# First attention of a four-layer network: value products ahead of the products for the maxima

## The chip, the cores and the metric

The kernel runs on one core of a Trainium2 chip. The metric is the device time of one execution in microseconds. A core has five engines with a program each: TensorE (PE, its weight loads are listed apart as PEld), VectorE (DVE), ScalarE (ACT), GpSimd (POOL) and SyncE (SP), which here only issues DMAs. The engines meet at semaphores alone, and each works through its program in the order in which it is written. TensorE writes to PSUM, which has eight banks of 128 x 512 float32.

## The reference, cut to what matters

Four layers, each `x = x + s * silu(f)` with an attention or a recurrence for `s` and a mixture of experts or a table of weights for `f`, both from the layer norm of `x`. The change lies in the attention of the first layer (2 batches of 1024 tokens, 16 heads, 8 numbers in a query or key, 64 in a value):

```python
cp = leaky_relu(einsum('btd,cd->btc', xn, Wc) + bc)
q, k, v = ...
scores = einsum('bqhd,bkhd->bhqk', q, k) / SCALE
attn = softmax(scores, axis=-1)
out = einsum('bhqk,bkhd->bqhd', attn, v).reshape(B, T, V_DIM)
proj = leaky_relu(einsum('btv,dv->btd', out, Wo) + bo)
s = xn + proj
```

## The kernel before, in words

The first attention is a loop of 256 iterations (`SCHED`, line 53; TensorE's part in lines 835 to 867). An iteration takes one group of four heads, one pair of heads in it, 512 queries and one tile of 128 keys. Eight iterations (the eight key tiles) make a **unit**: one pair of heads and 512 queries, 32 units in all. In iteration `i` TensorE issues, in this order:

- the **scores** of iteration `i`, four bf16 matmuls of 64 x 64 x 512 into a pair of PSUM banks, lines 846 to 852. ScalarE turns the pair into exponentials in SBUF (line 1916), which empties it;
- the products for the **maxima**: the softmax subtracts a row maximum, and these are found eight iterations and more ahead, by the same scores computed a second time with the queries on the partitions. `max_pair` (743 to 760) issues four bf16 matmuls of the same shape into another pair of banks, and VectorE reduces that pair to its maxima (1260), which empties it. `searched` (663 to 668) deals out 240 such pairs: one in each iteration up to 231, a second one in eight of the first 14 iterations (`EARLY`), none after 231;
- the **values** of iteration `i - 2` (`LAG`, line 44; `pv`, 783 to 800): four float32 matmuls of 64 x 64 x 512, exponentials times values, added up over the eight iterations of a unit in banks 6 and 7. `pv` waits for the exponentials of `i - 2`, and in the first iteration of a unit's sums also for banks 6 and 7 to be emptied, by ScalarE and by VectorE;
- `tails(i)` (802 to 833): in the second iteration of a unit the row sums of the unit before (16 float32 matmuls) and mostly the projection of the unit three back (8 float32 matmuls);
- what is left of `searched(i)`, and once in two units two small transposes for the maxima (`max_rows`, 762 to 774), in the fifth iteration of odd units.

The scores and the maxima take their banks from one ring of three pairs (0, 2, 4) in the order in which they are issued: `take` (379 to 382) hands out the next pair, and `vacant` (384) waits until what filled it last has been emptied. So the scores of `i` as a rule stand in the pair that the maxima of `i - 2` had, and wait for VectorE; the maxima of `i` stand in the pair that the scores of `i - 1` had, and wait for ScalarE. The tails and the transposes take a pair of the ring too.

VectorE's loop (1331 to 1346) reduces the pair of the iteration first; then come, once in a unit, additions of the low and high half of the values (`osb`, 1290) and of the projection (`acc_sb`, 1318) in the second iteration, the scaling of a finished unit by its reciprocal sums (`on_sb`, 1305) in the third, and a small sum with a reciprocal (1296 to 1298) in the sixth. GpSimd adds up exponentials for the row sums. Beside the loop all engines have parts of the layer's experts and of the next layer's routing, dealt out by iteration in `SIDE_B` (115 to 147); on VectorE these are for instance eight additions of an expert's rows to `gT`.

Of the kernel before, what the change touches and what calls it, by code (L numbers as in the profile page):

```python
# [43 lines left out]
LAG = 2  # L44
# [297 lines left out]
class Marks:  # L342
# [19 lines left out]
    def up(self, *keys, by=1):  # L362
        name = keys[0][0]
        self.n[name] = self.n.get(name, 0) + by
        self.named(name, self.n[name], [k for k in keys if len(k) > 1])
        return self.sem(name), by
# [4 lines left out]
    def at(self, *key):  # L371
        assert key in self.place or not self.known, key
        name, n = self.place.get(key, ("none", 0))
        return self.sem(name), n
# [4 lines left out]
    def take(self, ring):  # L379
        i = self.turn.get(ring, 0)  # L380
        self.turn[ring] = i + 1
        return ring[i % len(ring)]

    def vacant(self, b):
        return self.sem(f"bank{b}_empty"), self.n.get(f"bank{b}_full", 0)

    def filled(self, b, *keys):
        name = f"bank{b}_full"
        self.n[name] = self.n.get(name, 0) + 1
        self.named(name, self.n[name], keys)  # L390
        for k in keys:
            self.bank[k] = b
        return self.sem(name), 1
# [55 lines left out]
def _program(nc, A, out, ctx):  # L449
# [213 lines left out]
    def searched(i):  # L663


        done = min(i + sum(j < i for j in EARLY), 16 * (NBL - 1))
        to = min(i + 1 + sum(j <= i for j in EARLY), 16 * (NBL - 1))
        return [(1 + t // 16, t % 16) for t in range(done, to)]

    def rows_of(i, step):  # L670

        return i // 16 + 1 if i % 16 == MS[i >= 16] + step and i // 16 + 1 < NBL else None
# [16 lines left out]
    def tensor_program(pe):  # L689
# [53 lines left out]
        def max_pair(B, m, banks):  # L743

            g, pr = B // 2, B % 2
            s, qt, hk = g % 3, m // 2, m % 2
            for b in banks if len(banks) > 1 else (banks[0], banks[0] + 1):
                pe.wait_ge(*vacant(b))
            pe.wait_ge(*at(f"stack{s}_in", g))
            for a in range(2):  # L750
                r = slice(64 * a, 64 * a + 64)
                b = banks[a] if len(banks) > 1 else banks[0] + a
                for n in range(2):
                    ins = pe.mm(ps[64 * n:64 * n + 64, b, :],
                                Qs[r, s, 2 * pr + a, 128 * qt + 64 * n:128 * qt + 64 * n + 64],
                                Ks[r, s, pr, 512 * hk:512 * hk + 512])
                if len(banks) > 1:
                    ins.then_inc(*filled(b, ("mx", B, m, a)))
            if len(banks) == 1:
                ins.then_inc(*filled(banks[0], ("mx", B, m)))  # L760

        def max_rows(B, b):
            k = B % 2
            pb = ps[:, b, :].bitcast(BF16)
            pe.wait_ge(*vacant(b))
            pe.wait_ge(*at("rows_split", B))
            if B == 0:
                pe.tr(pb[0:48, 0:128], nsp[:, 0:48], identb).then_inc(*filled(b, ("rowsT", B)))
                return
            pe.wait_ge(*vacant(b + 1))  # L770
            for n in range(2):
                r = slice(64 * n, 64 * n + 64)
                ins = pe.tr(ps[:, b + n, :].bitcast(BF16)[0:48, 0:64], nsp[r, 48 * k:48 * k + 48], identb[r, r])
            ins.then_inc(*filled(b, ("rowsT", B)))
# [8 lines left out]
        def pv(i):  # L783
            g, pr, hf, kt = SCHED[i]
            tile = 8 * (g // 4) + kt
            if kt == 0:
                pe.wait_ge(*vacant(6))
                pe.wait_ge(*vacant(7))
            pe.wait_ge(*at("exp", i))
            for n in range(2):  # L790
                r = slice(64 * n, 64 * n + 64)
                for a in range(2):
                    h = 4 * (g % 4) + 2 * pr + a
                    ins = pe.mm(ps[64 * a:64 * a + 64, 6 + n, :],
                                V0[r, 1024 * tile + 64 * h:1024 * tile + 64 * h + 64],
                                Ps[r, i % NP, 512 * a:512 * a + 512], start=kt == 0, stop=kt == 7)
                if kt == 7:
                    ins.then_inc(*filled(6 + n, ("pvd" if n else "pvd_low", i)))
            if kt < 7:
                ins.then_inc(*up(("pvd", i)))  # L800
# [29 lines left out]
        def tails(x):  # L830
            unit_tail(x // 8 - 3, x % 8 + 16)
            unit_tail(x // 8 - 1, x % 8)
            unit_tail(x // 8 - 2, x % 8 + 8)

        def attention():
            ring[0] = (0, 2, 4)
            for b in range(8):
                pe.wait_ge(*vacant(b))
            pe.wait_ge(*at("v", 0, 1))
            for i, (g, pr, hf, kt) in enumerate(SCHED):  # L840
                s, b0 = g % 3, take(ring[0])
                pe.wait_ge(*vacant(b0))
                pe.wait_ge(*vacant(b0 + 1))
                pe.wait_ge(*at("rows0_in", 2 * g + pr))
                pe.wait_ge(*at("rows1_in", 2 * g + pr))
                for a in range(2):
                    r = slice(64 * a, 64 * a + 64)
                    for n in range(2):
                        ins = pe.mm(ps[64 * n:64 * n + 64, b0 + a, :],
                                    Ks[r, s, pr, 128 * kt + 64 * n:128 * kt + 64 * n + 64],  # L850
                                    Qs[r, s, 2 * pr + a, 512 * hf:512 * hf + 512])
                ins.then_inc(*filled(b0, ("st", i)))
                pairs = searched(i)
                for p in pairs[:1]:
                    max_pair(*p, (take(ring[0]),))
                if i >= LAG:
                    pv(i - LAG)
                tails(i)
                for p in pairs[1:]:
                    max_pair(*p, (take(ring[0]),))  # L860
                if rows_of(i, AFTER[i >= 16]):
                    max_rows(rows_of(i, AFTER[i >= 16]), take(ring[0]))
                yield
            pv(254)
            pv(255)
            for x in range(256, 260):
                tails(x)
# [274 lines left out]
        def down_ffn(q):  # L1142
            layer = GROUPS[q][0]
            wide, chunks = HIDDEN[layer], HIDDEN[layer] // 128
            for J in range(FIRST[q], FIRST[q + 1]):
# [6 lines left out]
                for k in range(halves(J)):  # L1152
# [9 lines left out]
                  "ffn2": ffn2, "tile": tile, "att3": att3, "state3": state3, "end3": end3, "route": route}  # L1162
        follow(ORDER_A["tensor"], stages)
        beside(attention(), SIDE_B["tensor"], stages)
        ring[0] = (4, 6, 7)
        follow(ORDER_C["tensor"], stages)
# [1550 lines left out]
```

## Time and profile before

| what | us |
|---|---|
| median of 3 runs (lowest, highest) | 989.15 (988.64, 989.76) |
| the profiled execution, its own time | 985.0 |
| its span, from first to last instruction | 983.2 |
| first and last exponential of the loop start | 152.4 and 607.1 |
| busy in the span: PE, DVE, POOL, ACT | 894.0, 766.7, 599.2, 537.4 |

The profile shows one execution, 4.15 us below the median of the runs; 1.8 us of its time lie outside its span. Busy time of PE counts a matmul from its start to a modelled end, and matmuls overlap, so a busy PE need not be at its limit. "Idle before" is the time that an engine, or TensorE's weight loading, did nothing before an instruction, with the work whose end released it.

### The profile page before, as it was taken

What the parts mean: (1) busy time and instruction counts of PE and PEld (TensorE: products, weight loads), DVE (VectorE), ACT (ScalarE), POOL (GpSimd) and SP (SyncE); (2) the same over time, 40 slices, a digit from 0 to 9 for tenths busy, and PEclk for the clock granted to TensorE, in tenths of its full rate; (3) what the DMA queues carried; (4) which work ended last, traced back from release to release, by engine and by line L of the source; (5) the groups of instructions that cost most, each with busy time, mean ns of one, the idle gap of its engine ahead of it and who ended that gap; (6) DMA issues with size and microseconds to landing.
All of it is one profiled execution on the core that took longest, in us unless ns stands there. A gap on an engine that the chain in (4) does not pass through costs nothing. (4 is left out here: it accounts for less than half of the span.)

```text
span 983.2 us, 20738 instructions
## 1 busy us (share of the span) xinstructions
PE 894.0 (91%) x7627; PEld 471.3 (48%) x7627; DVE 766.7 (78%) x1324; ACT 537.4 (55%) x903; POOL 599.2 (61%) x533
## 2 busy tenths in 40 slices
PE   4899997999999999899998999789999778799996
PEld 2356562233333333233332233679887444478695
DVE  6997789888888888998888852894589999983413
ACT  2154455666766676566666676454365334375463
POOL 3670327668887776878698876106527787572323
PEclk9899998999999999999999999999999999999999
DMA  9362364011111201102111113548761001253562
GB/s 314 117 208 86 105 195 145 16 41 47 32 57 29 65 25 31 49 22 74 40 40 38 40 35 110 169 140 262 217 188 62 23 24 52 68 164 106 161 180 83
DMA packets 90339, 94.86 MB, mean 96 GB/s; under 512 B 23136, under 2 KB 67296, under 8 KB 89984
## 3 DMA queue, kind: packets, MB, share of 16 engines
q1 hardware_dynamic: 85120, 83.04, 27.5%
q0 software_dynamic: 5120, 10.50, 3.7%
q8 instruction: 62, 1.02, 0.4%
q14 instruction: 37, 0.30, 0.1%
HBM read 68.79 MB, written 24.25 MB: 95 GB/s over the span
## 5 line engine op out<-in xcount | busy, mean ns | idle before, releaser
L254 PE MATMUL ps<-ar 64*64 64x512 f32 (+3 forms) x5244 | 518.7, 446 | 28.1 <-DVE small L276 8.9
L254 PEld LDWEIGHTS ps<-ar 64*64 64x64 f32 (+2 forms) x5244 | 254.3, 135 | 275.7 <-ACT ar L300 84.1
L300 ACT ACTIVATE ar<-ps 128x1024 f32<-128x1024 f32 (+1 forms) x302 | 284.0, 944 | 117.5 <-PE ps L254 111.3
L276 DVE TENSOR_REDUCE small<-ps 128x2 f32<-128x1024 f32 (+2 forms) x276 | 306.6, 1139 | 46.6 <-PE ps L254 44.7
L263 POOL TENSOR_TENSOR psum_sb<-psum_sb,ar 128x1024 f32<-128x1024 f32 x91 | 214.8, 2360 | 53.1 <-DVE on_sb L263 41.9
L263 POOL TENSOR_TENSOR ar<-ar 128x512 f32<-128x512 f32 (+1 forms) x80 | 80.0, 1004 | 45.4 <-DVE ar L276 22.3
L322 POOL DMA_INDIRECT gT<-ysort,rt x48 | 48.0, 999 | 92.8 <-issue 91.5
L263 DVE TENSOR_TENSOR ar<-ps,ar 128x256 f32<-128x256 f32 (+4 forms) x48 | 50.5, 1059 | 55.2 <-PE ps L254 51.4
L263 POOL TENSOR_TENSOR psum_sb<-ar 128x1024 f32<-128x1024 f32 x32 | 75.8, 2370 | 23.8 <-ACT ar L300 16.6
L297 ACT COPY ar<-ps 128x256 f32<-128x256 f32 (+2 forms) x84 | 30.8, 378 | 72.7 <-PE ps L254 33.3
L254 PE MATMUL ps<-wA,xnT 128*128 128x512 f32 (+3 forms) x208 | 60.8, 419 | 4.0 <-DVE rt L268 1.8
L254 PE MATMUL ps<-ar,onesf 128*32 128x512 f32 x384 | 61.0, 593 | 1.4 <-DVE psum_sb L263 1.3
L254 PEld LDWEIGHTS ps<-ar,psum_sb 128*128 128x128 f32 x428 | 52.1, 192 | 7.8 <-issue 7.5
L254 PE MATMUL ps<-ar,psum_sb 128*128 x428 | 55.3, 276 | 0.2 <-DVE psum_sb L263 0.2
L297 ACT COPY lrow<-ps 128x512 f32<-128x512 f32 x32 | 18.8, 586 | 66.8 <-PE ps L254 66.8
L317 POOL DMA_INDIRECT xsort<-ar,rt x32 | 35.7, 1115 | 30.4 <-DVE rt L279 22.3
L276 DVE TENSOR_REDUCE ar<-ar 128x16 f32<-128x256 f32 (+1 forms) x48 | 49.6, 1037 | 0.7
L317 POOL DMA_INDIRECT xsort<-acc_sb,rt x32 | 35.4, 1105 | 20.3 <-DVE rt L279 10.8
L254 PE MATMUL ps<-ar,ps_sb 128*128 x92 | 46.5, 604 | 0.0
L260 PE MATMUL ps<-cf,ar 128*128 128x128 f32 x256 | 33.1, 287 | 9.3 <-DVE acc_sb L271 5.0
L254 PEld LDWEIGHTS ps<-wA,xnT 128*128 128x128 f32 x208 | 30.8, 196 | 22.1 <-issue 9.7
L260 PEld LDWEIGHTS ps<-cf,ar 128*128 128x128 f32 x256 | 30.8, 149 | 14.5 <-DVE acc_sb L271 5.6
(160 smaller groups left out, 1077.2 us busy)
## 6 DMA issues: line engine op xcount, KB each, us to landing
ar<-in_L_up SPq DMA_DIRECT2D x46, 384.0 KB, 4.0
ar<-in_L_b SPq DMA_DIRECT2D x30, 322.0 KB, 3.6
rec_sb<-lscr SPq DMA_DIRECT2D x64, 128.0 KB, 2.9
scr<-ar SPq DMA_DIRECT2D x48, 128.0 KB, 2.6
ar<-xsort SPq DMA_DIRECT2D x36, 128.0 KB, 3.9
ysort<-ar SPq DMA_DIRECT2D x36, 128.0 KB, 1.9
ar<-scr SPq DMA_DIRECT2D x32, 112.0 KB
ar<-scr SPq DMA_DIRECT2D x32, 96.0 KB
```

Of the source, the lines that this page charges most:

```text
L254: return self.e.matmul(o, l, r, start=start, stop=stop) if self.e else Nothing()
L260: return self.e.matmul(o, i, idn, start=start, stop=stop, is_transpose=True) if self.e else Nothing()
L263: return self.e.tensor_tensor(o, a, b, op) if self.e else Nothing()
L276: return self.e.tensor_reduce(o, a, AX.X, op, negate=True) if negate else self.e.tensor_reduce(o, a, AX.X, op)
L297: return self.e.copy(o, a) if self.e else Nothing()
L300: return self.e.activation(o, a, fn, **kw) if self.e else Nothing()
L317: return self.e.indirect_dma_start(rows, bass.IndirectOffsetOnAxis(ap=index, axis=0), i, None)
L322: return self.e.indirect_dma_start(o, None, rows, bass.IndirectOffsetOnAxis(ap=index, axis=0))
```

## The change

In TensorE's program the call of `pv` moves ahead of the first pair of the iteration's maxima. Which work is done, in which banks and with which semaphores stays the same (the values take no pair of the ring), and no other engine's program changes.

```diff
                 ins.then_inc(*filled(b0, ("st", i)))
                 pairs = searched(i)
+                if i >= LAG:
+                    pv(i - LAG)
                 for p in pairs[:1]:
                     max_pair(*p, (take(ring[0]),))
-                if i >= LAG:
-                    pv(i - LAG)
                 tails(i)
                 for p in pairs[1:]:
                     max_pair(*p, (take(ring[0]),))
```

## Rows read from the trace of the kernel before

**Rows 1.** Page, busy time: us (share of the span) xinstructions.
```profile
PE 894.0 (91%) x7627; PEld 471.3 (48%) x7627; DVE 766.7 (78%) x1324; ACT 537.4 (55%) x903; POOL 599.2 (61%) x533
```

**Rows 2.** Busy time by stretch: PE, PEld, DVE, ACT, POOL, clock, DMA.
```profile
198.00:560.00 362.00, 350.07 (x3884) 111.03 (x3876) 314.80 (x394) 241.12 (x281) 285.36 (x216) 1.00 0.15 42
```

**Rows 3.** ScalarE in order of time, 295 to 310 us: one unit.
```profile
295.64 1.03 ACT L300 ACTIVATE ar<-ps 128x1024 f32<-128x1024 f32 x1 [0.30 <-PE ps L254]
...
301.25 2.16 ACT L300 ACTIVATE ar<-ps 128x1024 f32<-128x1024 f32 x2
303.87 1.03 ACT L300 ACTIVATE ar<-ps 128x1024 f32<-128x1024 f32 x1 [0.46 <-PE ps L254]
305.16 1.02 ACT L300 ACTIVATE ar<-ps 128x1024 f32<-128x1024 f32 x1 [0.26 <-PE ps L254]
306.48 1.03 ACT L300 ACTIVATE ar<-ps 128x1024 f32<-128x1024 f32 x1 [0.30 <-PE ps L254]
...
309.10 1.03 ACT L300 ACTIVATE ar<-ps 128x1024 f32<-128x1024 f32 x1 [0.30 <-PE ps L254]
```

**Rows 4.** ScalarE in the last iterations of the loop, without maxima.
```profile
606.05 1.03 ACT L300 ACTIVATE ar<-ps 128x1024 f32<-128x1024 f32 x1
...
607.12 1.02 ACT L300 ACTIVATE ar<-ps 128x1024 f32<-128x1024 f32 x1
```

**Rows 5.** TensorE's weight loads in order of time, from 300 us.
```profile
300.63 0.60 PEld L254 LDWEIGHTS ps<-ar 64*64 64x64 bf16 x16 [0.84 <-issue]
...
302.33 0.39 PEld L254 LDWEIGHTS ps<-ar 64*64 64x64 bf16 x12 [0.70 <-ACT ar L300]
...
304.94 0.39 PEld L254 LDWEIGHTS ps<-ar 64*64 64x64 bf16 x12 [0.51 <-ACT ar L300]
```

**Rows 6.** VectorE in order of time, 301 to 309 us, the same unit.
```profile
301.31 1.23 DVE L276 TENSOR_REDUCE small<-ps 128x2 f32<-128x1024 f32 x1 [1.38 <-PE ps L254]
302.45 0.68 DVE L263 TENSOR_TENSOR on_sb<-osb,rec_sb 128x512 f32<-128x512 f32 x1
303.05 1.22 DVE L276 TENSOR_REDUCE small<-ps 128x2 f32<-128x1024 f32 x1
304.18 1.22 DVE L276 TENSOR_REDUCE small<-ps 128x2 f32<-128x1024 f32 x1
...
306.55 0.16 DVE L276 TENSOR_REDUCE small<-lcol 128x8 f32<-128x16 f32 x1
...
306.87 2.38 DVE L276 TENSOR_REDUCE small<-ps 128x2 f32<-128x1024 f32 x2
```

**Rows 7.** All engines, 334 to 337 us, where VectorE is late.
```profile
334.29 1.36 DVE L271 SCALAR_TENSOR_TENSOR gT<-acc_sb,rt,gT 128x128 f32<-128x128 f32 x1
...
335.57 1.21 DVE L276 TENSOR_REDUCE small<-ps 128x2 f32<-128x1024 f32 x1
...
336.83 0.60 PEld L254 LDWEIGHTS ps<-ar 64*64 64x64 bf16 x16 [1.47 <-DVE small L276]
```

**Rows 8.** VectorE by groups, 198 to 572 us: busy us, mean ns, idle before.
```profile
L276 DVE TENSOR_REDUCE small<-ps 128x2 f32<-128x1024 f32 x208 | 248.1, 1215 | 37.8 <-PE ps L254 36.2
L263 DVE TENSOR_TENSOR on_sb<-osb,rec_sb 128x512 f32<-128x512 f32 x26 | 23.9, 919 | 0.0
...
L271 DVE SCALAR_TENSOR_TENSOR gT<-acc_sb,rt,gT 128x128 f32<-128x128 f32 x8 | 6.5, 807 | 0.0
```

**Rows 9.** TensorE's weight loads behind the transposes of an odd unit.
```profile
318.40 0.11 PEld L254 LDWEIGHTS ps<-ar 64*64 64x64 bf16 x4 [0.52 <-ACT ar L300]
318.91 0.39 PEld L254 LDWEIGHTS ps<-ar 64*64 64x64 bf16 x12 [0.40 <-DVE small L276]
```

**Rows 10.** GpSimd in order of time, behind the loop.
```profile
661.87 1.09 POOL L317 DMA_INDIRECT xsort<-ar,rt  x1 [21.66 <-DVE rt L279]
```

**Rows 11.** Busy time by stretch, in the columns of rows 2.
```profile
156.00:158.00 2.00, 1.80 (x16) 0.67 (x20) 2.00 (x3) 0.74 (x1) 1.98 (x2) 0.50 0.50 159
...
402.00:404.00 2.00, 0.05 (x4) 0.05 (x8) 1.97 (x4) 0.00 (x0) 1.37 (x2) 1.00 0.00 0
```

## The prediction

> **What bounds the kernel now.** The page comes first: TensorE is busy for 91% of the span, VectorE for 78% [rows 1]. That is an average over four layers, so the second view is the busy time by stretch. In the steady part of the first attention TensorE is busy for 350 of 362 us, VectorE for 315, ScalarE for only 241 [rows 2]. Third, the iterations one by one. From the start of one exponential to the next it is 1.29 or 1.32 us where nothing else is in the way [rows 3]. In the last iterations, which have no maxima, it is 1.07 [rows 4]. So the four bf16 matmuls of the maxima take 0.22. The scores are four matmuls of the same form, 0.22 as well, and 0.86 is left for the values. These three add up to 1.29 with nothing over: in a plain iteration TensorE's issue is the limit. Fourth, what TensorE waits for. The maxima of an iteration mostly come just behind the end of an exponential: their weights are loaded 0.51 us after the load before, released by ScalarE, and 0.70 in the iteration in which ScalarE also copies the row sums [rows 5]. The excess of 0.2 there, and the 0.03 in every second plain iteration, are what the old order loses to ScalarE. VectorE is no limit yet, but it is near: a unit of 13.46 us (from 295.64 to 309.10) [rows 3] holds eight reductions, each of which keeps it for 1.13 (303.05 to 304.18) [rows 6].
>
> **What is removed and what is added.** No instruction is. The four matmuls of the values with their eight weight loads, and the signals that they give, come 0.22 earlier in an iteration; the four matmuls of the maxima come 0.86 later. No DMA is issued in either, and no queue is passed.
>
> What is gained: the maxima no longer stand behind an exponential that has only just ended. Per unit that returns the 0.2 and about three times 0.03, together 0.29. In odd units there is one more: behind the transposes the maxima wait for VectorE; their weights come 0.51 behind the ones of the scores (318.40 to 318.91) [rows 9] where 0.22 is the issue, so 0.29 more is returned, as the values are now issued during that wait.
>
> What is lost: the maxima's pair of banks goes to the scores two iterations later. In the old order TensorE issues maxima, values, scores, maxima and values between the two: 0.22 + 0.86 + 0.22 + 0.22 + 0.86 = 2.38. In the new order it is maxima, scores, values and maxima: 0.22 + 0.22 + 0.86 + 0.22 = 1.52. In that time the pair has to be filled, reduced and given back. From the start of the maxima to the start of an idle VectorE's reduction it is 0.44: scores start at 300.63, the maxima 0.24 behind them (0.22, and some 0.02 because the weights are not loaded ahead after a pause; compare 1.32 with 1.29 [rows 3]), the reduction at 301.31 [rows 5, 6]. The reduction lasts 1.22 [rows 8]. From its end to the weights of the scores it is 0.05 (335.57 + 1.21 = 336.78, then 336.83) [rows 7]. Together 1.71. **The old order has 0.67 to spare; the new one is 0.2 short**, and whatever else VectorE does in a unit comes on top, since nothing is left to absorb it. That such a wait is real is seen in the old kernel where an addition to gT of 1.36 makes VectorE late: the scores stand until the reduction ends [rows 7].
>
> **The walk through one unit**, from the scores of its third iteration (time 0), where VectorE has been idle behind the tails [rows 6]; an iteration without a wait is 1.29, the maxima start 1.07 behind the scores, and a wait costs 0.02 more for the weights, as above.
> - Third: maxima 1.07, reduction 1.51 to 2.73. Behind it VectorE does the scaling, 0.92 on average [rows 8], and starts the next reduction 0.08 before its end.
> - Fourth: scores 1.29, maxima 2.36; their reduction starts only at 2.73 + 0.92 - 2 x 0.08 = 3.49 and ends at 4.71.
> - Fifth: the scores would start at 2.58 but need the first reduction, 2.73 + 0.05 = 2.78: wait 0.20. Maxima 3.88, reduction 4.62 to 5.84.
> - Sixth: would start at 4.10, needs 4.76: wait 0.66. Maxima 5.86, reduction 6.30 to 7.52; the small sum and the reciprocal put 0.32 (306.55 to 306.87) [rows 6] behind it.
> - Seventh: 6.08, needs 5.89, no wait. Maxima 7.15, reduction 7.76 to 8.98.
> - Eighth: 7.37, needs 7.57: wait 0.20. Maxima 8.67, reduction 9.11 to 10.33.
> - First of the next unit: 8.89, needs 9.03: wait 0.14. Second: 10.35, needs 10.38: wait 0.03. Then the projection, whose pair is that of the maxima just before: 0.05.
>
> Waits 1.28, four times 0.02 for weights, 1.36 in all. Against the 0.29 returned this is **+1.07 for an even unit**. In an odd unit the transposes take one of the waits and the other 0.29 is returned: **+0.78**. The tails of about 2.8 us that follow let VectorE catch up, so nothing is carried over. Maxima run in units 0 to 28. Units 0 and 1, with the second pairs, are bound by VectorE already; I take nothing for them (bounds -2 and +3). For 14 even and 13 odd units it is 14 x 1.07 + 13 x 0.78 = 25.1. Units in which side work stands on TensorE may lose less, the eight additions to gT [rows 8] will cost more than now; I let the two cancel.
>
> The other waits of the values: in a unit's third iteration they also need banks 6 and 7, emptied by VectorE's addition of osb, and the maxima are now queued behind that wait. It ends about 2.3 us after the maxima before it (0.44, one reduction, the addition), and the tails put some 3.1 us between, so I take nothing; without that cover it would be up to 0.7 per unit. The values need the exponentials of two iterations back, long done. After the loop the next layer's tokens are sorted only when VectorE has finished with the attention's output: GpSimd idles for 21.66 us before it [rows 10]. So what the loop loses, the end loses.
>
> The sum goes against the profiled execution, 985.0 (span 983.2 and 1.8 around it): 1010.1. The median of the runs is 4.15 above it, so I forecast 989.15 + 25 = **1014 us**.
>
> Bounds. Low: only the three bare shortages of 0.2 per unit, less 0.29, for 27 units: 0.3 x 27 = +8, 997. High: all VectorE's extra work in the chain paid on top of 0.2 for every two iterations (0.7 + 0.84 + 0.32, less 0.29, is 1.57 per unit, 42 in all): 1031.
>
> **TensorE's clock** is where a rule speaks for another size. The rows: the granted clock is 1.00, the higher level of 2.4 GHz, over the whole steady stretch [rows 2], also in a stretch of 2 us with TensorE busy for 0.05 [rows 11]; at the loop's start, after a pause, it was 0.50, the 1.2 GHz level [rows 11]. The Trainium skill (TensorE: Matmul & The Clock Gate, A second HAM failure mode: psum-queue depth-cycling) says that TensorE cycling through PSUM banks with small idle times between groups can make its clock swing between the levels, which would be the third rival below instead of no cost. By rows 11 the trace speaks against it here.
>
> **Rivals.**
> 1. Faster: the pair comes back in time after all, because the reduction waits less for TensorE than the 0.44 that I read; it decides at 0.44 - 0.2 = 0.24 us. Then only what is returned counts: 14 x 0.29 + 13 x 0.58 = 11.6, 978 us. For it: ScalarE's release is what ends most of the maxima's waits now [rows 5]. Against it: 0.44 was read with VectorE idle. 4%.
> 2. A wash: the returned waits and the shortage cancel within 2 us, 989. It needs VectorE's scaling and small sums to find room in the tails, while rows 6 show them in the middle of the unit. 5%.
> 3. The clock falls for a tenth of the loop, 36 us at half speed, so 36 more: 1050. 2%.
> 4. More is lost: side work on VectorE and longer scalings fall into the chain in full, the high bound, 1031. For it: gT's 1.36 in rows 7. 12%.
>
> **How the numbers follow.** The forecast has 77%. Slower is the forecast with rivals 3 and 4, 91%; the same is rival 2, 5%; faster is rival 1, 4%. A difference under 0.2%, about 2 us, can't be told from none. The range takes in the forecast's bounds, from 997 to 1029, and leaves rivals 1, 2 and 3 and half of 4 outside.
>
> **What would show it.** Right: idle time of weight loads that reductions (DVE small) end grows by some 25 us or more in the loop while that ended by ScalarE shrinks; the start of the maxima is no longer late; units of about 14.5 us where 13.46 stood, with one iteration of about 1.9; VectorE idle behind TensorE between reductions. Wrong: units of 13.2, or waits at the values; a granted clock under 1.00 in the loop; a loop that got longer while the end did not move.

## The result, and the profile after

The changed kernel takes 1009.58 us (median of 4 runs, 1007.91 to 1011.51), the kernel before beside it 989.0: a ratio of 1.0206, with a 95% interval from 1.0183 to 1.023. It is slower by 20.6 us; 25 were forecast. The profiled execution took 1007.91, the fastest of the four, with a span of 1006.1. All times of "after" below are of that execution.

The page and the busy time by stretch come first, as [rows 1, 2] did. The columns of the stretch are those of rows 2.

```profile
PE 909.5 (90%) x7627; PEld 477.5 (47%) x7627; DVE 764.6 (76%) x1324; ACT 534.6 (53%) x903; POOL 595.9 (59%) x533
```

```profile
198.00:576.00 378.00, 358.85 (x3888) 111.85 (x3884) 312.39 (x398) 237.67 (x279) 284.31 (x216) 1.00 0.14 40
```

The counts of instructions are the same. The busy shares hardly move, and nobody could read the loss from them. The stretch tells it: 3888 matmuls take 378 us where 3884 took 362 [rows 2]. TensorE's busy time grew by 9 us with them, for nearly the same matmuls, whose ends are modelled; it is not read as more work. The granted clock is 1.00 as before, the level of 2.4 GHz.

ScalarE in order of time shows the iterations of one unit, to be set against [rows 3]. The columns are start, duration, engine, line, operation, and in brackets the idle time before it and its releaser.

```profile
301.39 1.02 ACT L300 ACTIVATE ar<-ps 128x1024 f32<-128x1024 f32 x1 [0.38 <-PE ps L254]
302.80 1.02 ACT L300 ACTIVATE ar<-ps 128x1024 f32<-128x1024 f32 x1 [0.39 <-PE ps L254]
...
307.08 2.16 ACT L300 ACTIVATE ar<-ps 128x1024 f32<-128x1024 f32 x2
309.74 1.03 ACT L300 ACTIVATE ar<-ps 128x1024 f32<-128x1024 f32 x1 [0.50 <-PE ps L254]
311.48 1.02 ACT L300 ACTIVATE ar<-ps 128x1024 f32<-128x1024 f32 x1 [0.71 <-PE ps L254]
312.76 1.03 ACT L300 ACTIVATE ar<-ps 128x1024 f32<-128x1024 f32 x1 [0.27 <-PE ps L254]
314.29 1.02 ACT L300 ACTIVATE ar<-ps 128x1024 f32<-128x1024 f32 x1 [0.50 <-PE ps L254]
315.70 1.02 ACT L300 ACTIVATE ar<-ps 128x1024 f32<-128x1024 f32 x1 [0.38 <-PE ps L254]
```

The unit lasts from 301.39 to 315.70, 14.31 us for 13.46. Four of its iterations carry the loss: 1.41 in the first (301.39 to 302.80), 1.74 (309.74 to 311.48), 1.53 (312.76 to 314.29) and 1.41 (314.29 to 315.70), where 1.29 to 1.33 stood. Next to them the weight loads of the scores and of the values, in order of time (those of the maxima, groups of four, are left out):

```profile
309.28 0.39 PEld L254 LDWEIGHTS ps<-ar 64*64 64x64 bf16 x12 [0.74 <-DVE small L276]
...
311.01 0.39 PEld L254 LDWEIGHTS ps<-ar 64*64 64x64 bf16 x12 [0.94 <-DVE small L276]
...
312.14 0.55 PEld L254 LDWEIGHTS ps<-ar 64*64 64x64 bf16 x12 [0.34 <-DVE small L276]
...
313.83 0.39 PEld L254 LDWEIGHTS ps<-ar 64*64 64x64 bf16 x12 [0.74 <-DVE small L276]
...
315.24 0.39 PEld L254 LDWEIGHTS ps<-ar 64*64 64x64 bf16 x12 [0.62 <-DVE small L276]
```

Each of these groups of twelve begins with the scores and is released by a reduction. In [rows 5] the groups of twelve began with the maxima and were released by an exponential. And VectorE, in order of time, against [rows 6]:

```profile
308.00 1.23 DVE L276 TENSOR_REDUCE small<-ps 128x2 f32<-128x1024 f32 x1 [1.71 <-PE ps L254]
309.14 0.68 DVE L263 TENSOR_TENSOR on_sb<-osb,rec_sb 128x512 f32<-128x512 f32 x1
309.74 2.35 DVE L276 TENSOR_REDUCE small<-ps 128x2 f32<-128x1024 f32 x2
312.55 1.23 DVE L276 TENSOR_REDUCE small<-ps 128x2 f32<-128x1024 f32 x1 [0.46 <-PE ps L254]
```

This is the ring closing on itself. Until 312.09 VectorE reduces without a pause while TensorE waits for it at 309.28 and 311.01; then VectorE idles 0.46 behind the very matmuls that it held up. Over the loop two waits grow, TensorE's for VectorE and VectorE's for TensorE, and one goes, TensorE's for ScalarE. The views group idle time by who waited, for whom, with total us, count and the longest; first before (152 to 612 us), then after (152 to 632 us).

```profile
PEld ps L254 <- DVE small L276: 85.1, 164, 2.5
PEld ps L254 <- ACT ar L300: 84.1, 172, 1.2
...
DVE small L276 <- PE ps L254: 39.1, 40, 2.0
```

```profile
PEld ps L254 <- DVE small L276: 136.6, 192, 2.6
...
DVE small L276 <- PE ps L254: 68.4, 103, 2.4
...
PEld ps L254 <- ACT ar L300: 10.3, 33, 1.2
```

The wait for ScalarE has gone from 84.1 to 10.3 us, and 51.5 have come to the wait for VectorE. (Weights are loaded while earlier matmuls still run, so these are not losses of time one for one.) Behind the loop nothing is caught up: the next layer's tokens are sorted 20.0 us later than in [rows 10], behind the same idle time.

```profile
681.90 1.09 POOL L317 DMA_INDIRECT xsort<-ar,rt  x1 [21.70 <-DVE rt L279]
```

### The profile page after: what moved, and what is told of

Same layout as the page of the kernel before. It is cut to its first block and busy times, and to the rows that moved or that the text cites. A ratio compares the mean times of both kernels' runs of the same rounds, so it can differ in the third digit from the quotient of the medians.

```text
span 1006.1 us, 20738 instructions
## 1 busy us (share of the span) xinstructions
PE 909.5 (90%) x7627; PEld 477.5 (47%) x7627; DVE 764.6 (76%) x1324; ACT 534.6 (53%) x903; POOL 595.9 (59%) x533
## 5 line engine op out<-in xcount | busy, mean ns | idle before, releaser
L254 PE MATMUL ps<-ar 64*64 64x512 bf16 (+3 forms) x5244 | 527.4, 447 | 29.7 <-DVE small L276 11.0
L254 PEld LDWEIGHTS ps<-ar 64*64 64x64 bf16 (+2 forms) x5244 | 255.8, 135 | 290.9 <-issue 119.2
L276 DVE TENSOR_REDUCE small<-ps 128x2 f32<-128x1024 f32 (+2 forms) x276 | 310.1, 1141 | 75.9 <-PE ps L254 74.4
L317 POOL DMA_INDIRECT xsort<-acc_sb,rt x32 | 33.0, 1032 | 20.3 <-DVE rt L279 10.8
L260 PE MATMUL ps<-cf,ar 128*128 128x128 f32 x256 | 35.7, 301 | 9.2 <-DVE acc_sb L271 5.0
L254 PEld LDWEIGHTS ps<-wA,xnT 128*128 128x128 f32 x208 | 30.5, 196 | 21.5 <-issue 6.8
L260 PEld LDWEIGHTS ps<-cf,ar 128*128 128x128 f32 x256 | 33.2, 158 | 14.5 <-DVE acc_sb L271 5.6
```

Source lines behind the costliest of these rows:

```text
L254: return self.e.matmul(o, l, r, start=start, stop=stop) if self.e else Nothing()
L260: return self.e.matmul(o, i, idn, start=start, stop=stop, is_transpose=True) if self.e else Nothing()
L276: return self.e.tensor_reduce(o, a, AX.X, op, negate=True) if negate else self.e.tensor_reduce(o, a, AX.X, op)
L317: return self.e.indirect_dma_start(rows, bass.IndirectOffsetOnAxis(ap=index, axis=0), i, None)
```

## The experiments

**Theory A** is the prediction's: the pair of banks of the maxima comes back late from VectorE. **Theory B**: the new order costs time on TensorE itself, whatever VectorE does, say by the change from float32 to bf16 and back at another place.

**1. Short reductions in the kernel before.** VectorE reduces half of each bank; the other half of the keys is left out of the maxima. The same edit is in the next run.

```diff
-                dve.red(negm[B % 2][:, m:32:16], ps[:, b:b + 2, :], ALU.max, negate=True).then_inc(
+                dve.red(negm[B % 2][:, m:32:16], ps[:, b:b + 2, 0:CW // 2], ALU.max, negate=True).then_inc(
```

> The kernel before, with VectorE reducing the first 256 of the 512 keys of each bank of a pair, half the elements; which maxima it leaves out matters only for how the exponentials are scaled. Theory A (the pair of banks comes back late from VectorE): in the old order VectorE has 0.67 us to spare, so even units stay at about 13.45 us; the first two units, which VectorE bounds, get some 6 us shorter in all, and the wait behind the transposes of odd units mostly goes (13.96 to 13.7): 978 to 983 us. Theory B (the new order costs on TensorE itself): the same for this kernel.

Measured: 976.05 us, a ratio of 0.9843 (0.9806 to 0.988) against the kernel before.

```profile
291.17 1.02 ACT L300 ACTIVATE ar<-ps 128x1024 f32<-128x1024 f32 x1 [0.27 <-PE ps L254]
...
304.63 1.02 ACT L300 ACTIVATE ar<-ps 128x1024 f32<-128x1024 f32 x1 [0.30 <-PE ps L254]
```

The even units with nothing else in them stay at 13.46 us (291.17 to 304.63), so in the old order VectorE does not set them. What is gained is in units 0 and 1 (28.3 for 32.7), in the odd units (13.67 for 13.96) and in units with work of other layers in them (13.67 for 14.55 in units 5, 7 and 9, 13.46 for 14.24 in 12 and 14).

**2. Short reductions in the changed kernel.**

> The new order, with the same halved reductions. Theory A: a reduction of about 0.69 us makes the chain 0.44 + 0.69 + 0.05 = 1.18 us, inside the 1.52 that the new order leaves, so the waits for VectorE vanish and what is left of the change is its gain: even units 13.1 to 13.2 us, 5 to 10 us less than the old order with halved reductions. Theory B: the loss has nothing to do with VectorE, units are 0.8 us longer than with the old order and halved reductions, some 20 us in all.

Measured: 973.79, a ratio of 0.9824 (0.979 to 0.9858) against the kernel before: with the same reductions the new order is no longer slower than the old one of run 1. VectorE's group of reductions first (count, busy us, mean ns, idle before), then ScalarE through one unit:

```profile
L276 DVE TENSOR_REDUCE small<-ps 128x2 f32<-128x512 f32 x207 | 142.5, 691 | 129.0 <-PE ps L254 127.5 <-issue 1.2
```

```profile
289.73 1.02 ACT L300 ACTIVATE ar<-ps 128x1024 f32<-128x1024 f32 x1 [0.27 <-PE ps L254]
...
302.88 1.03 ACT L300 ACTIVATE ar<-ps 128x1024 f32<-128x1024 f32 x1 [0.26 <-PE ps L254]
```

With a reduction of 0.69 us the unit lasts 13.15 us, 0.31 less than with the same reductions in the old order. That is the 0.29 which the prediction said the change returns, measured without the wait that covers it. B falls: the same TensorE program in the same order loses nothing. The total is only 2.3 us below run 1, where 5 to 10 were expected, and the executions of the two runs overlap (969.53 to 975.37 here, 971.54 to 979.89 there). What the units gain is given back elsewhere in the loop: 1.35 us in units 0 and 1, 1.3 each in units 17 and 23, 1.9 in units 28 and 29. Unit 23 can be read: the scaling took 2.85 us there, beginning 0.06 behind the start of an addition of GpSimd's (the last section has more of these), and the transposes then waited 2.29 for the reduction behind it. What the others wait for was not tried.

**3. Reductions of three quarters in the changed kernel** (`0:384` of each bank; the last quarter of the keys is left out). It asks whether the loss grows with the reduction's length or begins at a point.

> The new order, reductions over 384 of the 512 keys of each bank (the rest of the keys is left out of the maxima). Theory A: a reduction of 0.96 makes the chain 0.44 + 0.96 + 0.05 = 1.45 us, just inside 1.52: the bare shortages go, only the scaling still causes a wait of about 0.1: even units 13.2 to 13.4. If the loss fell in proportion to the length of the reduction instead, they would be at about 13.75 (half way between 14.31 and 13.15).

Measured, in one run: 989.22 us. The reduction takes 0.96 us, and ScalarE shows:

```profile
L276 DVE TENSOR_REDUCE small<-ps 128x2 f32<-128x768 f32 x203 | 193.4, 956 | 83.9 <-PE ps L254 81.7 <-issue 1.6
```

```profile
293.54 1.02 ACT L300 ACTIVATE ar<-ps 128x1024 f32<-128x1024 f32 x1 [0.27 <-PE ps L254]
...
301.53 1.03 ACT L300 ACTIVATE ar<-ps 128x1024 f32<-128x1024 f32 x1 [0.26 <-PE ps L254]
302.97 1.03 ACT L300 ACTIVATE ar<-ps 128x1024 f32<-128x1024 f32 x1 [0.41 <-PE ps L254]
...
306.84 1.03 ACT L300 ACTIVATE ar<-ps 128x1024 f32<-128x1024 f32 x1 [0.27 <-PE ps L254]
```

The unit is 13.30 us (293.54 to 306.84). Half of the way from 0.69 to 1.22 costs 0.15, the other half 1.01. So there is a point, as A has it: 0.44 + 0.96 + 0.05 = 1.45 still fits into the 1.52 that the new order leaves, 1.71 does not. The 0.15 stand in one iteration (301.53 to 302.97), the sixth, whose scores need the pair that is reduced behind the scaling. Runs 2 and 3 take work off VectorE as well; run 8 below leaves its work whole and gives the pair more time instead.

**4. Half of the scaling in the changed kernel** (half of the queries stay unscaled).

```diff
-                half = slice(512 * m, 512 * m + 512)
+                half = slice(512 * m, 512 * m + 256)
```

> The new order, with only the first half of a finished unit's columns scaled (the other half of the queries is left out). Theory A: the scaling takes 0.37 instead of 0.68 between two reductions; the long iteration of 1.73 shrinks by 0.3: even units 13.95 to 14.05, about 8 us less than the changed kernel. If the scaling is not in the chain: 14.31.

Measured, in one run: 1000.9 us, 8.7 below the changed kernel, and even units of 14.04 us. The iteration of 1.74 became 1.46:

```profile
308.86 1.02 ACT L300 ACTIVATE ar<-ps 128x1024 f32<-128x1024 f32 x1 [0.50 <-PE ps L254]
310.32 1.02 ACT L300 ACTIVATE ar<-ps 128x1024 f32<-128x1024 f32 x1 [0.44 <-PE ps L254]
```

No wait of TensorE ends with a scaling, yet 0.27 us less of it (0.41 for 0.68 in this unit) give 0.27 us in an even unit: what VectorE does between two reductions stands in the chain now. In an odd unit they give only 0.04 (14.47 for 14.51): the sixth iteration becomes 1.54 for 1.76, but the seventh 1.49 for 1.32. Units 2 to 28 are 5.0 us shorter together (400.6 for 405.6); that the total of this one execution came out 8.7 shorter, next to the expected 8, is in part luck.

**5. The scaling one iteration earlier in the changed kernel**, among the tails, where VectorE has time.

```diff
-            if k == 10:
+            if k == 9:
```

> The new order, with VectorE's scaling of a finished unit (on_sb) one iteration earlier, where VectorE idles behind the row sums. Theory A: the scaling no longer stands between two reductions, so the long iteration of 1.73 us in every unit shrinks to about 1.3 to 1.5, the bare shortages of 0.2 stay: about 0.4 us per unit, 27 units, some 11 us less than the changed kernel, 997 to 1001. Theory B: no difference, 1009.

Measured: 1009.6 us, a ratio of 1.0188 (1.0161 to 1.0214), so nothing was gained, and A missed. Half of it came true: even units with nothing else in them last 13.99 us, and the iteration of 1.74 is gone. Units 17, 23 and 28 got shorter by 1.3 to 2.1 as well. But other units got longer: 15.19 for 14.51 in units 5, 7 and 9, 16.0 for 15.17 in 12 and 14, 15.90 for 14.36 in 13 and 15.91 for 14.31 in 20. Unit 5 shows why for 5, 7, 9 and 20, with GpSimd, VectorE and the weight loads in order of time:

```profile
233.44 2.37 POOL L263 TENSOR_TENSOR psum_sb<-ar 128x1024 f32<-128x1024 f32 x1
```

```profile
233.64 2.72 DVE L263 TENSOR_TENSOR on_sb<-osb,rec_sb 128x512 f32<-128x512 f32 x1
236.29 0.67 DVE L263 TENSOR_TENSOR acc_sb<-acc_sb,ps 128x512 f32<-128x512 f32 x1
```

```profile
237.01 0.39 PEld L254 LDWEIGHTS ps<-ar 64*64 64x64 bf16 x12 [1.59 <-DVE acc_sb L263]
```

The scaling took 2.72 us where it takes 0.68 in this unit of the changed kernel. It began 0.20 behind the start of GpSimd's addition and ended 0.55 behind its end (235.81). Over 26 scalings the mean is 1.31 us in this run, 0.92 before [rows 8] and 0.82 after the change; of the 32 in the whole trace 19 began while GpSimd added here, 7 before and 2 after the change. So the moved step met another engine at its new place. In units 12 and 14 it was an addition to gT that met GpSimd (2.19 and 2.18 us for 0.90), and in unit 13 the granted clock fell (last section).

**6. Maxima between the two halves of the values, split by keys** (`between` issues the maxima when two of the four value matmuls are out).

```diff
-        def pv(i):
+        def pv(i, between=None):
...
             for n in range(2):
+                if n and between:
+                    between()
```

> The maxima between the two halves of the values: two value matmuls, the maxima, the other two. Theory A: from the maxima to the scores two iterations on there are now 1.95 us against the chain of 1.71, 0.24 to spare: only the scaling still causes a wait of about 0.2 per unit, while the waits for ScalarE are gone: even units 13.35 to 13.45, odd ones 13.4 to 13.6, in all 981 to 987. Theory B: the cost goes with how far the maxima are moved, half of the loss: about 999.

Measured: 1015.46 us, a ratio of 1.0263 (1.0227 to 1.0299). Both theories missed. The weight loads of this run, then VectorE:

```profile
314.48 0.78 PEld L254 LDWEIGHTS ps<-ar 64*64 64x64 bf16 x16 [0.95 <-DVE small L276]
```

```profile
316.02 1.23 DVE L276 TENSOR_REDUCE small<-ps 128x2 f32<-128x1024 f32 x1 [0.46 <-PE ps L254]
```

The scores start at 314.48 and the reduction of their iteration's maxima at 316.02, 1.54 later. In the changed kernel it is 311.01 and 312.55, 1.54 as well. So the maxima did not come any earlier, and the edit did not make what it was to test. In the trace the four value matmuls, on four quarters of the array, run side by side: they take 0.86 together, and the two of the first half alone hold their quarters as long as all four (314.72 to 315.58). Two of the maxima's four products need the same quarters, and the reduction needs all four products. The Trainium skill (TensorEngine Tiling (Array Packing), Key Properties) says that different tiles of the array can load and multiply in parallel; the trace agrees, with 0.86 for two as for four, and the values had to be split another way. Run 6 speaks neither for A nor for B. (Its odd units are longer than those of the changed kernel, 15.03 for 14.51; why was not tried. Its unit 17 is longer too, 19.62 for 18.05, with a granted clock of 0.50 from 421 to 423 us.)

**7 and 8. Maxima between two halves of the queries, in the old kernel.** Now each half takes all four quarters of the array for 256 queries. In 7 this is done only in the fourth iteration of all units and the sixth of the odd ones, where the old order loses to ScalarE or to the transposes; in 8 in all iterations but a unit's second and third (`i % 8 not in (1, 2)` for the condition in brackets). Both leave the first two units as they are.

```diff
             pe.wait_ge(*at("exp", i))
+            if between:
+                for c in (0, 256):
+                    for n in range(2):
...
+                            ins = pe.mm(ps[64 * a:64 * a + 64, 6 + n, c:c + 256],
...
+                    if c == 0:
+                        between()
...
-                for p in pairs[:1]:
-                    max_pair(*p, (take(ring[0]),))
-                if i >= LAG:
-                    pv(i - LAG)
...
+                if i >= 16 and pairs and (i % 8 == 3 or i % 16 == 13):
+                    pv(i - LAG, first)
```

> The old order, but in the fourth iteration of every unit and the sixth of odd ones (from iteration 16 on) the values are issued in two halves of 256 queries, all four tiles of the array in each, with the maxima between the halves. These are the two places where the old order waits (0.2 for ScalarE, 0.29 for VectorE behind the transposes). Theory A: the maxima are 0.43 us later instead of 0.86, VectorE's chain keeps 0.24 to spare, in the fourth iteration the reduction stands behind the scaling anyway: 0.17 to 0.2 per unit and 0.29 per odd unit come back, 14 x 0.2 + 13 x 0.45, some 8 us less than before: 980 to 983. Theory B (TensorE pays for leaving the old order, here by the second loads of the weights): no gain or a loss of a few us.

> The same halves in all iterations but the second and third of a unit (which keep the old order). Theory A: the bare shortage does not arise (0.24 to spare), the waits for ScalarE are gone, the scaling causes a wait of about 0.2: even units about 13.4, odd ones 13.4 to 13.6, 981 to 987 us. Theory B: the more iterations leave the old order the longer it gets, over 995.

Measured: 984.76 us, a ratio of 0.9955 (0.993 to 0.998), for 7, somewhat above what was expected, and 985.11, 0.9952 (0.9935 to 0.997), for 8, inside it. Both are faster than either kernel, by some 4.7 us against the one before (989.64 in these runs), and both intervals leave out no change. In 8 an even unit is:

```profile
293.55 1.02 ACT L300 ACTIVATE ar<-ps 128x1024 f32<-128x1024 f32 x1 [0.27 <-PE ps L254]
...
306.77 1.03 ACT L300 ACTIVATE ar<-ps 128x1024 f32<-128x1024 f32 x1 [0.27 <-PE ps L254]
```

13.22 us for 13.46 [rows 3], with all plain iterations at 1.29. Half a step of the values is 0.43: ahead of the maxima it is enough for ScalarE to finish, which returns the 0.2, and behind them it leaves the pair 1.52 + 0.43 = 1.95 us, more than the 1.71 that it needs. The wait for the scaling, which the expectation put at 0.2, is not in the trace: the unit is shorter than the 13.4 it named. As VectorE's work is whole in this run, it is the time left to the pair that decides, and not the amount of VectorE's work. Not all of the gain arrives. Units 24 and 28 are longer than before in 7 (14.82 and 14.81 for 14.39 and 14.58); why was not tried. In 8 units 17 and 25 last 18.56 and 19.68 us for 17.27 and 17.97 in 7, and there the granted clock fell in 8 (last section); in 7 it stayed at 1.00 in both units.

## Why the prediction was right, and where its terms were off

The forecast, slower by 25 us through the pair that VectorE gives back late, is what happened, at 20.6. What it named as the signs came: the idle time of weight loads behind reductions grew by 51.5 us (some 25 or more), units of 14.31 and 14.51 (about 14.5), one iteration of 1.74 (about 1.9). Point by point:

- **The bank pair, 1.71 us against 2.38 and 1.52.** Shown by runs 2 and 3: with the reduction shortened to 0.96 us the chain is 1.45 and the loss goes, at 1.22 it is there. The bare waits of 0.20 that the walk gave the fifth and the eighth iteration are 0.22 in the trace: the eighth begins 1.53 behind the seventh (312.76 to 314.29), which is 1.29, the 0.02 for the weights and 0.22.
- **The 0.29 returned per unit.** Shown by run 2 against run 1 (0.31). In the changed kernel it is spent at once: from the two exponentials behind the tails to the next it is 2.66 us (307.08 to 309.74), where 2.62 with the 0.2 of ScalarE in it stood (301.25 to 303.87 [rows 3]).
- **The scaling at 0.92 us: the term that was mis-sized.** It is a mean over short scalings of 0.68 and a few of 1.25 to 2.6. In the changed kernel they fall elsewhere against GpSimd's additions, and 24 of the 26 take 0.68:

```profile
L263 DVE TENSOR_TENSOR on_sb<-osb,rec_sb 128x512 f32<-128x512 f32 x26 | 21.2, 815 | 0.0
...
L271 DVE SCALAR_TENSOR_TENSOR gT<-acc_sb,rt,gT 128x128 f32<-128x128 f32 x8 | 5.3, 657 | 0.0
```

  With 0.68 the sixth iteration's wait is 0.42 instead of 0.66, and the same walk gives +0.83 for an even unit and +0.54 for an odd one. Measured are +0.85 (14.31 for 13.46) and +0.55 (14.51 for 13.96). The sum becomes 14 x 0.83 + 13 x 0.54 = 18.6, and units 2 to 28 grew by 18.1 (405.6 for 387.5, by their exponentials). The unit that was walked had its 0.68 in [rows 6]; the mean was the wrong row. Run 4 shows the size for even units: 0.27 us hang on 0.27 of scaling. In odd units the same 0.27 gives only 0.04, so that 0.54 agrees with 0.55 there shows less. A longer scaling is paid in full in an odd unit too: of the two long ones that are left one is in unit 23, and with its 2.70 us, 2.02 more than 0.68, the sixth iteration is 3.78 us, 2.02 more than the 1.76 of a plain odd unit.
- **Units 0 and 1: taken as nothing, +2.2 measured** (34.8 for 32.7 us), inside the bound of +3. So the total errs by less than its terms: 6.5 too much for the scaling, 2.2 too little here. They were called bound by VectorE. VectorE was busy for 30.5 of the 33 us from 152 to 185 before, and is for 28.8 after, so it got gaps that it did not have. First before, then after:

```profile
152.00:168.60 16.60, 13.16 (x136) 4.30 (x140) 15.61 (x14) 8.09 (x8) 15.05 (x10) 0.79 0.45 137
168.60:185.00 16.40, 14.55 (x166) 4.35 (x162) 14.90 (x17) 9.55 (x11) 10.62 (x10) 1.00 0.19 60
```

```profile
152.00:168.60 16.60, 12.79 (x124) 3.90 (x116) 14.35 (x13) 8.06 (x8) 14.87 (x9) 0.79 0.45 138
168.60:185.00 16.40, 13.20 (x146) 3.82 (x146) 14.47 (x17) 8.42 (x10) 10.07 (x9) 1.00 0.16 54
```

- **Odd units and side work.** Letting the two cancel was right within a microsecond (19.1 from the plain units, 14 x 0.85 + 13 x 0.55, against 18.1), by differences of both signs. Units 5, 7 and 9 lost nothing (14.51 for 14.55), units 12 and 14 lost 0.93, and unit 23 lost 2.5 (16.48 for 13.96), by its long scaling. The additions to gT did not get longer (0.657 us for 0.807 [rows 8]).
- **Banks 6 and 7, taken as nothing:** right; from the third iteration's exponential, behind the tails, to the next it stayed 1.13 us.
- **The end moves with the loop:** right, by the 20.0 us of the sorting above.
- **The clock, left as it was:** right, 1.00 over the stretch. The rule on queue cycling in the Trainium skill (TensorE: Matmul & The Clock Gate, A second HAM failure mode: psum-queue depth-cycling), which would have made the third rival, speaks of such a pattern, small idle times between groups of matmuls that change banks. The trace does not agree: with all the waits for reductions from 198 to 576 us the granted clock stayed at 1.00.
- **The rivals.** The first (0.44 is too much) falls with the reduction at 312.55, before which VectorE idled 0.46: the scores before it start at 311.01, the maxima 0.24 + 0.86 behind them, at 312.11, and that leaves the 0.44. The second falls with 20.6. The third falls with the clock. The fourth, all of VectorE's extra work in the chain at its full price, is 21 above what was measured. (Its bound was worked out as 1031; the range ends at 1029, and nothing hangs on the difference.)

B, the theory against which the runs were made, is refuted by run 2. Where the returned time of runs 2, 7 and 8 is lost again is read for unit 23 of run 2 and units 17 and 25 of run 8 alone; the rest stays open.

## What to carry to other kernels

Before a step is moved past another, count for every buffer of the ring the time from filling it to its next use, in the old order and in the new, and set it against fill, reduction and return; a wait that goes can hide that the next one is 0.2 us away. If it does not fit, move half of the step: here that turned +20.6 into -4.7 us. And take an instruction's duration from the place where it runs, not as a mean over places with other neighbours; a step moved on one engine meets the others' timetable as well.

## What the runs showed of the hardware that was not expected

A product of two operands in SBUF on VectorE took 0.68 us alone and 2.72 while GpSimd added, and ended only after GpSimd's addition had (run 5). The Trainium skill (SBUF — State Buffer, SBUF: two separate sides) says that a VectorE operation with two SBUF inputs and a GpSimd operation that reads SBUF share a pair of ports, that the first to start keeps it for its whole instruction, and that the other fully blocks. The traces agree: in the ten traces 73 scalings began while one of GpSimd's additions into psum_sb ran, and every one ended behind it, 71 of them by 0.55 to 0.57 us whether they took 0.68 or 2.85, the two half scalings of run 4 by 0.28. It is read side by side; no run took the addition away. The wait stands in the profile as a longer instruction, with no idle time in front of it.

A hole in TensorE's work was followed by a lower clock in some places and not in others. In run 5 VectorE's addition to gT took 2.19 us in unit 12, and TensorE waited for the reduction behind it:

```profile
343.60 2.19 DVE L271 SCALAR_TENSOR_TENSOR gT<-acc_sb,rt,gT 128x128 f32<-128x128 f32 x1
```

```profile
346.97 0.39 PEld L254 LDWEIGHTS ps<-ar 64*64 64x64 bf16 x12 [2.77 <-DVE small L276]
```

Stretches of that run, in the columns of rows 2:

```profile
344.00:347.00 3.00, 0.93 (x16) 0.14 (x8) 3.00 (x3) 0.91 (x1) 2.62 (x2) 1.00 0.12 33
347.00:350.00 3.00, 3.00 (x24) 1.15 (x28) 1.95 (x3) 1.31 (x2) 1.99 (x6) 0.59 0.56 164
```

TensorE was busy for 0.93 of 3 us at a clock of 1.00, and the next 3 us ran at 0.59 on average, mostly at the level of 1.2 GHz. In run 8 it was busy for 1.30 of the 3 us from 399 and for 0.43 of those from 521, and the clock was 0.50 from 402 to 405 and from 525 to 528, in units 17 and 25; run 1 and run 3 show the same in unit 25 (19.13 and 19.53 us for 17.99). The hole of 2 us in [rows 11], at the same place of unit 17, had no such result, nor had one in unit 25 of the kernel before, with TensorE busy for 0.69 of the 2 us from 526. What decides between them these rows do not show.
